# Bias tiles of the late regions on DVE, a shorter lag between row and bias tiles, and the opening's matrix work on POOL and ScalarE

## The reference, cut to what matters

```python
# x: (1, 16, 1024, 1024) float32; c, L_mult, init_L: scalars; W1: (1, 32), W2: (32, 16)
rel = tril(q - k)                                       # distance, 0 above the diagonal
pos = maximum(rel.max(axis=-1), abs(L_mult * init_L))   # one number for each row q
nd = log(abs(c * rel) + 1) / (log(abs(c * pos) + 1) + 1e-6)
h = relu(nd[..., None] * W1[0] + b1)                    # 32 hidden values for each (q, k)
x = x + (h @ W2 + b2).transpose(2, 0, 1)                # a bias for each of the 16 channels

ret = einsum('BGMTS,GMN->BGNTS', x, w + eye)            # 16 channels mixed at each (t, s):
ret += rank-2 term of qw1, qw2 (differs by row t) + x * qdd[t]
ret += rank-2 term of kw1, kw2 (differs by column s) + x * kdd[s]
```

## Time and profile before

| | us |
|---|---|
| median of 3 runs | 1018.52 (1011.3 to 1022.31) |
| profiled execution: its time | 1017.06 |
| profiled execution: its span | 1015.1 |
| busy PE / ACT / DVE / POOL | 755.0 / 453.8 / 373.5 / 344.3 |
| mean granted TensorE clock, share of full speed | 0.89 |

### The profile page before, as it was taken

The page is one execution under the profiler, slowest core; times in us unless marked ns, Lnnn a source line. Parts: engine busy times, 40 slices in busy tenths (PEclk is TensorE's granted clock), DMA queues, the critical chain, the costliest instruction groups (busy, mean ns, idle before and its releaser), DMA issues.

```text
span 1015.1 us, 37021 instructions
## 1 busy us (share of the span) xinstructions
PE 755.0 (74%) x17186; PEld 545.3 (54%) x17186; DVE 373.5 (37%) x358; ACT 453.8 (45%) x472; POOL 344.3 (34%) x189
## 2 busy tenths in 40 slices
PE   2269697688767796697965978777796687867973
PEld 1029654486536753485534955347553485534963
DVE  7970265205640274204541045310354103541041
ACT  6554264444553263443653435534264443653400
POOL 7461044202440053202863027630276402771000
PEclk9679988798979997789999989979899798996997
DMA  6974799844997178943899138892388923790079
GB/s 112 204 163 82 191 201 238 191 103 107 226 205 175 41 164 214 200 107 85 179 203 201 47 85 183 206 191 49 83 154 211 200 67 79 168 214 3 5 161 194
DMA packets 366437, 149.50 MB, mean 147 GB/s; under 512 B 99660, under 2 KB 366028, under 8 KB 366284
## 3 DMA queue, kind: packets, MB, share of 16 engines
q1 hardware_dynamic: 229068, 80.02, 39.3%
q10 hardware_dynamic: 137216, 67.13, 27.6%
HBM read 77.61 MB, written 69.47 MB: 145 GB/s over the span
## 4 chain that ended last, share of the span: by engine, by line
PE 42%; SPq 15%; ACTq 15%; ACT 9%; issue 8%; DMA 4%; POOL 3%; DVE 3%; POOLq 0%; DVEq 0%
PE main L609 22%; ACTq L196 15%; PE main L599 11%; PE bias L622 9%; SPq L223 9%; ACT hidden L376 4%; SPq L230 4%; POOL hidden L339 3%; ACT hidden L371 3%; DMA mats_a<-a_mats 3%; ACT y L385 2%; DVE mixed L510 1%; DMA a_mats<-mixed 1%; DMA b_mats<-mixed 1%; DVE y L523 1%
## 5 line engine op out<-in xcount | busy, mean ns | idle before, releaser
L339 POOL TENSOR_TENSOR hidden<-log_table,row_scale 128x1024 f32<-128x1024 f32 x176 | 340.1, 1950 | 573.4 <-PE bias L622 560.7
L376 ACT ACTIVATE hidden<-hidden,b_col 128x1024 f32<-128x1024 f32 x176 | 197.6, 1144 | 293.6 <-issue 153.5
L622 PE MATMUL bias<-hidden,w_blocks 128*64 128x512 f32 x768 | 229.9, 714 | 129.2 <-ACT hidden L376 84.3
L510 DVE TENSOR_TENSOR mixed<-main,mixed 128x1024 f32<-128x1024 f32 x128 | 156.7, 1224 | 440.0 <-PE main L599 440.0
L599 PEld LDWEIGHTS main<-y,mats_a 32*32 32x32 f32 x8192 | 241.9, 131 | 121.2 <-issue 58.4
L599 PE MATMUL main<-y,mats_a 32*32 32x128 f32 x8192 | 271.3, 280 | 42.1 <-DMA mats_a<-a_mats 28.0
L609 PE MATMUL main<-y,mats_b 32*32 32x128 f32 x8192 | 258.0, 281 | 51.1 <-issue 37.8
L609 PEld LDWEIGHTS main<-y,mats_b 32*32 32x32 f32 x8192 | 243.3, 132 | 74.4 <-issue 46.5
L398 ACT ACTIVATE mixed<-main 128x1024 f32<-128x1024 f32 x128 | 130.9, 1023 | 199.5 <-PE main L609 194.2
L622 PEld LDWEIGHTS bias<-hidden,w_blocks 128*64 128x64 f32 x768 | 54.8, 155 | 233.5 <-issue 189.3
L523 DVE SCALAR_TENSOR_TENSOR y<-bias,b_col,x_stage 128x1024 f32<-128x1024 f32 x64 | 82.2, 1284 | 142.7 <-PE bias L622 142.7
(11 more groups left out here) (37 smaller groups left out, 27.5 us busy)
## 6 DMA issues: line engine op xcount, KB each, us to landing
x_stage<-in_x SPq DMA_DIRECT2D x512, 128.0 KB, 5.3
out_mixed<-mixed ACTq DMA_DIRECT2D x256, 128.0 KB, 4.4
out_mixed<-mixed ACTq DMA_DIRECT2D x128, 256.0 KB
mats_a<-a_mats SPq DMA_DIRECT2D x256, 32.0 KB
b_mats<-mixed SPq DMA_DIRECT2D x2, 512.0 KB, 6.1
mats_b<-b_mats SPq DMA_DIRECT2D x8, 128.0 KB, 2.8
a_mats<-mixed SPq DMA_DIRECT2D x2, 512.0 KB, 9.5
mixed<-in_L_conv_kw SPq DMA_DIRECT2D x2, 128.0 KB, 2.6
```

Source lines behind the costliest of these rows:

```text
L339: nc.gpsimd.tensor_tensor(hidden_tile(h).rearrange("p (j s) -> p j s", j=ROWS), bass.AP(logs.tensor, logs.offset, [list(logs.ap[0]), [1, R ...
L376: nc.scalar.activation(hidden_tile(h), hidden_tile(h), ACT.Relu, bias=b1_col[:, 0:1])\
L510: dve.tensor_tensor(at, main[:, T % 2, :].rearrange("p (t s) -> p t s", t=ROWS), at, ALU.add).then_inc(main_taken, 1)
L622: mm = pe.matmul(bias[into, T % 2, at:at + BANK], w2_blocks[:, g, :], hidden_tile(hidden_index(k, T, g))[:, at:at + BANK], start=True, sto ...
```

## The change

- `LAG` is 2 instead of 4. ScalarE makes the hidden tiles 0 and 1 in steps 0 and 1, none in step 2, and tile s - 1 in each further step, and does so ahead of the stores of the step instead of behind them. The pieces' stores stand in the same steps as before.
- Of the tiles with g = 1 in regions 4 to 7 each odd one (`by_dve`: T % 2 == 1) is made by DVE, 8 instructions max(log x scale, -b1), directly before `add_bias` of the tile before it. It is not made by POOL or ScalarE, and `row_by_row` is gone. As relu(z + b1) = max(z, -b1) + b1, the missing W2 b1 is put into the bias column that DVE adds for such tiles (`b2_col[:, 2]`), by one more matmul of one column in the opening. TensorE waits for these tiles on a semaphore of their own.
- Opening: DVE makes only the column matrices. POOL makes the row matrices, in five parts, behind its hidden tiles 1, 3, 5, 7 and 9. ScalarE copies both transposed results out of PSUM (tiles 3 and 13), and TensorE transposes the row matrices at tile 12 instead of 6. SP issues the x chunks 6 and 7 before it loads the column matrices. DVE inverts the later scales behind tiles 4 and 6 instead of both behind 2.

The diff, cut to its core (declarations of semaphores, moved helpers and plain renamings are left out):

```diff
-LAG = 4
+LAG = 2
...
-        def row_by_row(k, T, g):
-
-            return groups_of(k) == 2 and g == 1 and T % 4 == 3
...
+        def by_dve(k, T, g):
+
+            return groups_of(k) == 2 and g == 1 and T % 2 == 1
...
@@ sync
             for q in range(2, XSLOTS):
                 load_x(q)
             save_mats("b")
+            for q in range(XSLOTS, XCHUNKS):
+                load_x(q)
             sp.wait_ge(mats_out["b"], 2 * DMA)
             sp.wait_ge(mats_zeroed, 3)
             load_mats_b()
-            for q in range(XSLOTS, XCHUNKS):
-                load_x(q)
             save_mats("a")
@@ gpsimd
+            def compact_part(i):
+
+                if i == 0:
+                    pool.wait_ge(weights_in["a"], 4 * DMA)
+                    rank_one(nc.gpsimd, "a", 0, comp["a"]).then_inc(pool_step, 1)
+                    steps[0] += 1
+                elif i == 1:
+                    step(rank_one(nc.gpsimd, "a", 1, term["a"]))
+                elif i == 2:
+                    step(nc.gpsimd.tensor_tensor(comp["a"], comp["a"], term["a"], ALU.add))
+                elif i == 3:
+                    pool.wait_ge(eye_added, 1)
+                    whole = comp["a"].rearrange("p (b f) -> p b f", b=BLOCKS)
+                    step(nc.gpsimd.tensor_tensor(whole, whole, w_eye.unsqueeze(1).to_broadcast([P, BLOCKS, H * H]), ALU.add))
+                else:
+                    on = diagonal(comp["a"], BLOCKS)
+                    nc.gpsimd.tensor_tensor(on, on, diag["a"].rearrange("p (b m) -> p b m", b=BLOCKS), ALU.add)\
+                        .then_inc(comp_made["a"], 1)
...
-                        if row_by_row(k, T, g):
+                        if by_dve(k, T, g):
                             continue
...
+                    if k == 0 and T % 2 == 1 and T < 10:
+                        compact_part(T // 2)
@@ scalar
+            def take_turned(part):
+                for half in range(2):
+                    act.wait_ge(main_ready, half + (1 if part == "b" else 3))
+                    nc.scalar.activation(turned[part][:, half * COLS:(half + 1) * COLS], main[:, half, :], ACT.Copy)\
+                        .then_inc(main_taken, 1)
...
+                if T == 3:
+                    take_turned("b")
+                if T == 13:
+                    take_turned("a")
...
                 for s in range(TILES + LAG):
+                    if k + 1 < REGIONS:
+
+                        U = s if s < 2 else s - LAG + 1
+                        if U < TILES and s != LAG:
+                            make_hidden(k + 1, U)
+                        U = s - LAG
+                        if groups_of(k + 1) == 1 and U >= 0 and U % XTILES == XTILES - 1:
+                            add_const_bias(k + 1, U)
                     for i, spread in enumerate(SPREAD):
...
-                    if k + 1 < REGIONS:
-                        U = s - LAG + 1
-                        if 0 <= U < TILES:
-                            make_hidden(k + 1, U)
-                        U = s - LAG
-                        if groups_of(k + 1) == 1 and U >= 0 and U % XTILES == XTILES - 1:
-                            add_const_bias(k + 1, U)
@@ vector
+            dve.wait_ge(weights_in["a"], 4 * DMA)
+            eye = diagonal(w_eye, 1)
+            dve.tensor_scalar(eye, eye, 1.0, None, ALU.add).then_inc(eye_added, 1)
...
                 if groups == 2:
+                    base = 2 if by_dve(k, T, 1) else 0
                     dve.scalar_tensor_tensor(out=y_rows(slice(0, P), row, ROWS), in0=falling(T % 2, 0, 0, P, ROWS),
-                                             scalar=b2_col[:, 0:1], in1=x_rows(slice(0, P), k, T, 0, ROWS),
+                                             scalar=b2_col[:, base:base + 1], in1=x_rows(slice(0, P), k, T, 0, ROWS),
...
+            def make_hidden(k, T):
+
+                h = hidden_index(k, T, 1)
+                dve.wait_ge(hidden_used, h - RING + 1)
+                dve.wait_ge(scales_in, DMA)
+                t0 = k * W + T * ROWS
+                for j in range(ROWS):
+                    at, of_row = t0 - SLOTS * W + j, (t0 + j) % PART
+                    one = dve.tensor_scalar(hidden_tile(h)[:, j * W:(j + 1) * W], log_table[:, at:at + W],
+                                            row_scale[:, of_row:of_row + 1], neg_b1[:, 0:1], ALU.mult, ALU.max)
+                one.then_inc(dve_hidden_ready, 1)
...
                     if U is not None and k + 1 < REGIONS:
+                        if U + 1 < TILES and by_dve(k + 1, U + 1, 1):
+                            make_hidden(k + 1, U + 1)
                         add_bias(k + 1, U)
@@ tensor
-            pe.matmul(bias[high_half, 1, 0:1], w2_blocks[:, 1, :], relu_b1[:, 0:1], start=True, stop=True)\
+            pe.matmul(bias[high_half, 1, 0:1], w2_blocks[:, 1, :], relu_b1[:, 0:1], start=True, stop=True)
+            pe.matmul(bias[high_half, 1, 1:2], w2_blocks[:, 1, :], b1_col[:, 0:1], start=True, stop=True)\
...
-                pe.wait_ge(hidden_ready, hidden_index(k, T, groups - 1) + 1)
+                pe.wait_ge(hidden_ready, made_through(k, T, groups - 1, False))
+                if by_dve(k, T, groups - 1):
+                    pe.wait_ge(dve_hidden_ready, made_through(k, T, 1, True))
...
                     transposes("b")
-                if T == 6:
+                if T == 12:
                     transposes("a")
```

More of the change, by code:

```diff
@@ L197, in store_block, with wait_x_slot, load_x_block, rank_one @@
                                  of_block(mixed, W * W, b, mixed_place(first_row) * W, [[2 * W, n], [1, W]]))
+        def wait_x_slot(eng, q):
+            if q >= XSLOTS:
+                eng.wait_ge(y_ready, (q - XSLOTS + 1) * XTILES)
+                if (q - XSLOTS) // XCHUNKS < HALF:
+                    eng.wait_ge(y_const_ready, q - XSLOTS + 1)
+        def load_x_block(eng, q, b):
+            slot = q % XSLOTS
+            t0 = q // XCHUNKS * W + q % XCHUNKS * XROWS
+            eng.dma_start(of_block(x_stage, XSLOTS * XROWS * W, b, slot * XROWS * W, [[1, XROWS * W]]),
+                          x[0, :, t0:t0 + XROWS, b * W:(b + 1) * W]).then_inc(x_in[slot], DMA)
         def phase_steps():
             return [(s if s < TILES else None, s - LAG if s >= LAG else None) for s in range(TILES + LAG)]
+        def rank_one(eng, part, i, dst):
+            shape = [P, BLOCKS, H, H]
+            u = first[part].rearrange("p (b i m) -> p b i m", b=BLOCKS, i=2)[:, :, i, :]
+            v = second[part].rearrange("p (b i m) -> p b i m", b=BLOCKS, i=2)[:, :, i, :]
+            return eng.tensor_tensor(dst.rearrange("p (b m n) -> p b m n", b=BLOCKS, m=H),
+                                     u.unsqueeze(3).to_broadcast(shape), v.unsqueeze(2).to_broadcast(shape), ALU.mult)
+        def diagonal(ap, blocks):
+            return bass.AP(ap.tensor, ap.offset, [list(ap.ap[0]), [H * H, blocks], [H + 1, H]])
         block = ctx.enter_context(nc.Block())
@@ L214, in load_x @@
             def load_x(q):
[L215 to L221, removed]
+                wait_x_slot(sp, q)
                 for b in range(BLOCKS):
[L223 to L224 removed]
+                    load_x_block(sp, q, b)
             def load_mats_a(q):
@@ L363, in make_hidden @@
                 for g in range(groups_of(k)):
[L364 to L375, removed]
+                    if not by_dve(k, T, g):
+                        h = hidden_index(k, T, g)
+                        act.wait_ge(nd_ready, made_through(k, T, g, False))
                         nc.scalar.activation(hidden_tile(h), hidden_tile(h), ACT.Relu, bias=b1_col[:, 0:1])\
                             .then_inc(hidden_ready, 1)
+            def take_turned(part):
[3 more added lines that the diff above has]
+                        .then_inc(main_taken, 1)
             def add_const_bias(k, T):
@@ L502, in _ @@
             dve.wait_ge(const_bias_read, 1)
-            compact("b")
+            step(dve.tensor_copy(b2_col[:, 2:3], b2_col[:, 0:1]))
+            dve.tensor_tensor(b2_col[P // 2:, 2:3], b2_col[P // 2:, 0:1], bias[P // 2:, 1, 1:2], ALU.add)\
+               .then_inc(const_bias_read, 1)
+            step(dve.tensor_scalar(neg_b1[:], b1_col[:], -1.0, None, ALU.mult))
+            compact_columns()
+            dve.wait_ge(weights_in["a"], 4 * DMA)
+            eye = diagonal(w_eye, 1)
+            dve.tensor_scalar(eye, eye, 1.0, None, ALU.add).then_inc(eye_added, 1)
             def finish_tile(k, T):
```

76 lines of the change are left out of this document (30 added, 46 removed).

## The result

The changed kernel is slower: 1063.18 us median of 4 runs (1051.51 to 1083.05) against 1018.69; ratio 1.0361, 95% interval 1.0251 to 1.0471. Its runs took 1051.51, 1057.46, 1068.91 and 1083.05 us at mean granted clocks of 0.885, 0.874, 0.868 and 0.859, and the last two, over 1.5% longer than the first, are left out of the ratio. The profiled execution took 1051.51 us, span 1049.3, which is 34.2 us more than the one of before. The forecast was 1017 us with a range of 958 to 1048, and a chance of 0.27 for slower.

A forecast was written before the change was run, and what follows sets the result against it. No engine was taken to bound the kernel throughout; late row phases lose time at head and tail. Opening 0, early phases +5 -4 -6, DVE's turns -15, clock +8, stores +12 sum to 0: 1017 us, own range 1003 to 1033 (958 to 1048 wider).

The forecast's parts named there:

- Part 1: Late row phases: lag 2 and ACT's new order give 70 us, 20 less in each of four, if DVE's part is free.
- Part 2: Late row phases: DVE's tiles and POOL's products take turns, 10.8 us a pair, 86.4 a phase, -15 in four.
- Part 3, the clock: Late row phases: TensorE's waits of 2.9 us a pair can drop its clock; 2 us a phase (0 to 10), +8.
- rival B: Late row phases: the clock falls in every pair, 9.6 us a phase instead of 2, 1047 us in all; chance 0.17.
- Part 3, the stores: Start of late column phases: the last stores land late, PE waits 2 to 3 us; +3 each, +12 (0 to +20).
- Part 4, SP's order: Early row phases: an x chunk goes ahead of row matrices; region 0 +5 us, region 1 -4, region 2 -6.
- Part 5, the opening: Opening: POOL making the row matrices leaves its end near 78 us, now 77.0; 0 (-6 to +12).

The follow-up runs named there:

- e_early: The changed kernel with DVE making its tile ahead of its addition for the row tile, not behind it; 960.14 us, ratio 0.9446.
- u_dve: The changed kernel with DVE's tiles undone, ScalarE making every fourth second-group tile row by row as before; 966.05 us, ratio 0.9506.
- p_pool: The changed kernel with POOL multiplying only 8 of the 128 positions of each row in regions 4 to 7; 961.33 us.
- f_first: The changed kernel with TensorE running the first group's two matmuls before it waits for DVE's tile; 1028.26 us.
- u_lag: The changed kernel with lag 4 and ScalarE's old order (stores first), DVE's tiles and new opening kept; 1071.54 us.
- p_xsmall: e_early with every x load of regions 1 to 7 cut to 1 of its 16 rows, same number of DMAs; 885.34 us.
- u_open: e_sp with the opening of before the change; 937.88 us against 949.56 for e_sp on the same chip.
- e_sp: e_early with the row matrices loaded ahead of the second x chunk in SP's queue; 942.67 us, and 949.56 the second time.

## Why the prediction was wrong

It took the right mechanism and the wrong one of its cases. By its own parts, in the profiled executions:

- **Part 1** (what lag 2 brings if DVE's part is free: late phases of 70): right, 69 to 72 in e_early, 72 to 73 in u_dve.
- **Part 2** (the turns; 10.8 us a pair, DVE's tile 5.5): right in the middle of a phase, 10.6 and 5.35, with the 3 + 1 + 1 + 3 of the instructions as placed. p_pool and e_early show the cause. Wrong at the end: I let DVE's last tile, 15, run free, "bias 1.9 beside DVE's last tile". In three of the four phases POOL makes three products around it, the tile takes 5.7 us, and TensorE waits up to 5.47 us for it. It weighed little: f_first, with the clock out of the sum, has 352 us in four phases where my working had 346. The single instruction, put at 0.29 us, takes 0.34 and is spaced 0.26 (three in 0.85).
- **Part 3, the clock, is the step that failed.** I took 2 us a phase out of 0 to 10, "while shorter gaps often cost nothing", and put the clock in every pair down as rival B at 0.17. f_first shows 40 us in four phases, 10 each, the upper end, and 32 more than I had: almost the whole 34.5 by which the profiled execution missed the forecast (the median is 46 off). The other terms that were off cancel, which is luck: the early row phases came out 14 us shorter than I had them, the column phases 7 longer, the pairs and tails without the clock 7 longer, the opening and the last row phase 1 each. What I had was one gap at a time; the pairs repeat a wait of 2.9 us every 10.6. Rival B's 96 us a phase (86.4 and 9.6) is what was measured (96 to 99), though as 31 us in the 24 pairs, for its 38, and 9 behind the last row tiles. Its total of 1047, 4.5 us off the profiled 1051.5, rests on the same luck.
- **Part 3, the stores**: the wait was there (ScalarE waited 34 us for `out_mixed`), but TensorE lost only 1.4 us to it. The column phases grew all the same, by 19 us, where I had 12, for another reason. u_lag shows that the growth goes with the lag and ScalarE's order, and p_xsmall, on e_early, that traffic beside such phases stretches them: 41 MB in all in the changed kernel against 31 before. I had said that they are left alone.
- **Part 4, SP's order**: region 1's row tile 12 at 44 us, forecast 44, and the phases -5.9 and -7.3 against -4 and -6. Region 0 came out at -5.7 instead of +5: I added the full 9.5 us of an x chunk to its row tile 12, which started 49.7 us into the phase instead of 57.7 (48.2 before), and what follows it took 21.8 us instead of 24.5.
- **Part 5, the opening**: 78.3 against 77.0 us to the first column phase, as forecast, but its end is not where its cost ends. u_open puts the cost at about 12 us in e_sp, the upper end of what I gave, most of it where I did not look for it. In the changed kernel itself it wasn't measured.

## What to carry to other kernels

When work moves to DVE in SBUF-to-SBUF instructions, lay its place in DVE's queue against POOL's instructions before its length: the same eight instructions cost 2.5 us when they began late in POOL's last product and 5.35 us when they began 0.7 us before its next two, and one place in a program was worth 9% of the kernel. Price a repeated wait of TensorE with the clock at its dearer end: here 99 us of waits, 32 of some 3 us each, cost 40 us more in clock. And look at what the traffic of a shortened phase does in the next one; a phase that an edit doesn't touch can still pay for it.

## What the runs showed of the hardware

- In the changed kernel POOL's waiting product goes ahead of DVE's next queued instruction, also where DVE's are only 0.26 us apart: in 31 of the 32 runs of eight (the last one met only the end of one product) exactly one passes between two products. DVE's own additions with one input in PSUM stayed at 1.21 to 1.29 us beside POOL, and POOL's products beside DVE's eight at 1.90.
- Two groups of matmuls that write to different column halves overlap entirely: 1.94 us for both, 1.93 for one.
- TensorE's gaps in the column phases that the waits put down to "issue" follow DMA traffic, and they end where instructions arrive. The page of the changed kernel has a DMA queue for instructions (packets, MB, share of the 16 engines):

```profile
q8 instruction: 134, 2.20, 1.0%
```

Of the 34 gaps, 68 us in all, 31 end 1.3 to 1.7 us after a 16 KB packet of this queue has landed; the other three, of 4 to 5 us, stand before the first column tile of a region. Without such ones the gaps are 53 us in the changed kernel, 38 before the change, 51 in e_early and 9 in p_xsmall, which has as many of these packets. By this timing TensorE waits there for instructions, which come over the same DMA engines as the data, and waits longer when these are busy; no run varied the instructions' traffic by itself.
